# Causal attention beside a mixture of experts: the places of the next head group's maxima within a group

## The chip, the cores and the metric

The kernel runs on one core of a Trainium2 chip. The time is the device time of one execution in microseconds (us). Three runs of the kernel before gave 526.77 us (median), 525.68 and 532.72.

## The reference, cut to what matters

The input has 2 sequences of 1024 tokens with 256 features. It is layer-normalised; causal attention with 16 heads of 16 features and an ALiBi bias, and a mixture of 16 experts (2 per token) with one shared expert, are both computed from the normalised tokens and added to the input. The attention is the part that matters here:

```python
scores = jnp.einsum('bqhd,bkhd->bhqk', q, k) * scale
bias = alibi_slopes[:, None, None] * rel
causal = pos[None, :] <= pos[:, None]
scores = jnp.where(causal[None, None], scores + bias[None], NEG)
attn = jax.nn.softmax(scores, axis=-1)
out = jnp.einsum('bhqk,bkhd->bqhd', attn, v).reshape(b, s, d)
out = out @ out_w.T + out_b
```

The softmax subtracts the exact maximum of each query's row of scores. So the scores are computed twice: once for the maxima, once (transposed) for the exponentials.

## The kernel before, in words

The first 235 us or so are projections, routing and experts. Then comes the attention, which works in 8 **groups** of 4 heads (2 sequences with 4 groups each). All that the change touches lies in this part, in the bodies of the eight groups.

**A group's scores.** A group is 12 steps, one per pair of a query half (512 queries) and a key block (128 keys): steps 0 to 3 have the first half, steps 4 to 11 the second. Each step has 4 heads, so there are 48 head steps; I write 9.2 for head 2 of step 9. `exp_scores` (line 1226) issues for each the matmul of line 1234 into one of three PSUM banks, and on a diagonal block the mask matmul of line 1237 too. ScalarE takes the exponential (line 718) and frees the bank, so TensorE can be at most three head steps ahead of it. The blocks on the diagonal get narrower: 512, 384, 256 and 128 columns in steps 0 to 3 and again in steps 8 to 11; steps 4 to 7 are full, 512 columns without a mask.

**A group's weighing.** After the last head of steps 2, 4, 6, 8 and 10, `weigh` (line 1240) multiplies the exponentials of the two steps before with the values (line 1248). I call these W2 to W10: W8 weighs steps 6 and 7, W10 weighs steps 8 and 9. The last two steps of a group are weighed either after step 0 of the next group or, at the end of each pair of groups, right behind step 11.

**The maxima of the next group.** While group g is being scored, TensorE also computes the plain scores of group g+1 in 27 pieces, p0 to p26 (`max_scores`, line 1205; matmuls of line 1222, mask of line 1223). Pieces p3 to p6 are 384 wide, p7 to p10 512, p11 to p14 640, p15 to p18 768, p19 to p22 896 and p23 to p26 1024; p0 to p2 hold several short rows. VectorE reduces each to its maximum (line 970). There are two places in PSUM for pieces, so piece n waits until VectorE has read piece n-2. The 28th item, p27, is the transpose of all the maxima (line 1213), which I call T. It waits for the maximum of p26. VectorE negates its result and splits it into three bf16 parts (lines 978 to 985), SyncE's queue stores these as three more rows of the queries (`store_neg`, line 454), and the first score of group g+1 waits until they have landed (`pe.wait_ge(s_nl[par], ...)` in `pair`).

**What sets the order.** `schedule()` makes one list, `ORDER`, which TensorE and VectorE both follow. It puts the 48 head steps in a row, each with a cost of its columns and 230 more. The pieces get places in three windows, given as shares of the group's total cost: p3 to p10 of group g+1 in the first, p11 to p27 of group g+1 in the second, and p0 to p2 of group g+2 in the third. VectorE's own list holds only the pieces in their order, so it doesn't change when the shares do.

Of the kernel before, what the change touches and what calls it, by code (L numbers as in the profile page):

```python
# [57 lines left out]
NP = len(PIECES) + 1  # L58
NBUF = 4
RING = 6  # L60
EARLY = 3


def schedule():
# [6 lines left out]
    pieces = []  # L71
    for (ahead, ps), (start, end) in WINDOWS:
        cost = [(1 + PIECES[p][0]) * P * PIECES[p][2] + 200 if p < NP - 1 else 100 for p in ps]
# [3 lines left out]
    for item, cost in zip(items, exp_cost):  # L77
# [4 lines left out]
        while pieces and pieces[0][0] <= now:  # L82
# [3 lines left out]


FIRST_HALF = 11
WINDOWS = [((1, range(EARLY, FIRST_HALF)), (0.0, 0.2)), ((1, range(FIRST_HALF, NP)), (0.22, 0.88)),
           ((2, range(EARLY)), (0.9, 1.0))]  # L90
OUT_AFTER = 3
ORDER = schedule()

# [1234 lines left out]
```

## Time and profile before

| | |
|---|---|
| three runs | 526.77 us median (525.68 to 532.72) |
| the profiled execution | 528.23 us, its span 526.4 us |
| TensorE busy | 457.2 us, 87% of the span |
| VectorE busy | 324.8 us, 62% |
| ScalarE busy | 246.4 us, 47% |
| GpSimd busy | 198.5 us, 38% |
| first score of group 0 | 241.90 us |
| first score of group 7 | 466.17 us |

The busy time of TensorE counts a matmul until its modelled end, which lies up to 0.16 us after the next one has begun. So a wait shorter than that doesn't show as idle time; it shows as a larger distance between two starts. A matmul of 512 columns that is followed at once by another has its successor 0.22 us later, though its own row says 0.38.

### The profile page before, as it was taken

To read this page: it belongs to the slowest core of one execution; us is meant where nothing else is said; L and a number is where in the kernel's file an instruction comes from. 1 tells how busy PE (TensorE), PEld (TensorE's weight loads), DVE (VectorE), ACT (ScalarE), POOL (GpSimd) and SP (SyncE) were. 2 spreads that over 40 slices of the span, in tenths; PEclk is the share of its full clock that TensorE was granted. 3 is DMA by queue.
4 is the path that set the end of the run, shared out by engine and by line. 5 is a ranking of instruction groups with operands and counts; after the bars stand their busy time and mean duration, and the time that the engine had idled before them with its cause. 6 is when DMAs were issued, how large, how long until landed. Compare 5 with 4: busy or idle time off the path is not lost.

```text
span 526.4 us, 9031 instructions
## 1 busy us (share of the span) xinstructions
PE 457.2 (87%) x3049; PEld 274.7 (52%) x3050; DVE 324.8 (62%) x610; ACT 246.4 (47%) x567; POOL 198.5 (38%) x239
## 2 busy tenths in 40 slices
PE   4595999639778999978989999799998999989998
PEld 4454888416545666754444354344444444332676
DVE  4869985413344656576767768677686767744232
ACT  2620652112122333324757668486675757768300
POOL 3470777699940000008888888600000000000000
PEclk9699799978779999996999999999999999999999
DMA  8898998799997333424114333221120000010022
GB/s 279 187 403 254 324 323 284 238 159 168 201 187 180 116 116 123 131 71 136 42 44 118 103 84 106 65 80 46 53 77 16 3 2 3 1 12 7 3 87 75
DMA packets 65704, 64.60 MB, mean 123 GB/s; under 512 B 21934, under 2 KB 59538, under 8 KB 65634
## 3 DMA queue, kind: packets, MB, share of 16 engines
q1 hardware_dynamic: 51506, 47.85, 30.8%
q0 software_dynamic: 13056, 15.83, 14.3%
q10 hardware_dynamic: 1104, 0.41, 0.3%
q8 instruction: 24, 0.39, 0.3%
q14 instruction: 14, 0.11, 0.1%
HBM read 37.27 MB, written 27.13 MB: 122 GB/s over the span
## 4 chain that ended last, share of the span: by engine, by line
PE 66%; DMA 15%; DVE 10%; issue 2%; SPq 2%; POOL 2%; ACT 2%; POOLq 0%; DVEq 0%
PE ps L1248 11%; PE ps L1234 11%; PE ps L1222 11%; PE ps L1147 7%; PE ps L1043 6%; DMA x_in<-sorted_tokens 6%; PE ps L1268 5%; PE ps L1163 4%; DVE mx L970 4%; DMA ks<-aux_rows 2%; SPq L454 2%; PE ps L1237 2%; PE ps L1223 2%; PE ps L1137 2%; DMA qs<-nr 2%
## 5 line engine op out<-in xcount | busy, mean ns | idle before, releaser
L718 ACT ACTIVATE pt<-ps 128x512 f32<-128x512 f32 (+3 forms) x384 | 163.9, 496 | 86.7 <-PE ps L1237 66.9
L970 DVE TENSOR_REDUCE mx<-ps 128x1 f32<-128x384 f32 (+6 forms) x189 | 153.9, 863 | 59.3 <-PE ps L1223 59.0
L1248 PE MATMUL ps<-pt,vg 128*32 128x512 f32 (+3 forms) x768 | 72.1, 492 | 0.0
L575 POOL DMA_INDIRECT yg<-sorted_outputs,slot_i x32 | 32.0, 999 | 95.7 <-DMA sorted_outputs<-y_out 86.9
L1147 PE MATMUL ps<-w_gu,hx 128*128 x192 | 57.8, 428 | 4.4 <-issue 3.3
L1234 PE MATMUL ps<-qs,ks 111*128 111x512 bf16 (+3 forms) x192 | 55.2, 332 | 4.4 <-DMA qs<-nr 4.4
L1234 PE MATMUL ps<-qk 111*128 111x512 bf16 (+3 forms) x192 | 54.1, 328 | 3.9 <-DMA qk<-nr 2.8
L935 DVE COPY y_out<-ps 128x256 f32<-128x256 f32 x48 | 20.4, 425 | 53.9 <-PE ps L1163 48.8
L1237 PE MATMUL ps<-cbf 128*128 128x128 bf16 x256 | 52.4, 221 | 0.0
L1222 PE MATMUL ps<-qk 108*128 108x512 bf16 (+3 forms) x192 | 50.1, 328 | 0.8 <-DVE mx L970 0.6
L691 ACT ACTIVATE hx<-ps 128x384 f32<-128x384 f32 (+1 forms) x48 | 22.9, 478 | 59.2 <-PE ps L1137 56.5
L1223 PE MATMUL ps<-cbf 128*128 128x128 bf16 x224 | 47.7, 225 | 0.0
L1147 PEld LDWEIGHTS ps<-w_gu,hx 128*128 128x128 f32 x192 | 36.3, 210 | 14.0 <-issue 9.4
L542 POOL DMA_INDIRECT sorted_tokens<-xn,slot_i x32 | 32.9, 1027 | 25.1 <-DVE slot_i L877 15.7
L1222 PE MATMUL ps<-ks,qs 108*128 108x512 bf16 (+3 forms) x144 | 39.4, 341 | 1.3 <-DVE nrf L980 0.7
L547 POOL COPY vg<-v_sb 128x512 f32<-128x512 f32 x8 | 4.9, 622 | 93.1 <-PE ps L1248 93.1
L1248 PEld LDWEIGHTS ps<-pt,vg 128*32 128x32 f32 x768 | 19.6, 109 | 32.9 <-ACT pt L718 17.7
L1163 PE MATMUL ps<-w_dn,hx 128*128 x96 | 33.4, 431 | 1.3 <-ACT hx L691 0.9
L1234 PEld LDWEIGHTS ps<-qk 111*128 111x128 bf16 x192 | 17.9, 97 | 25.3 <-issue 7.8
L590 POOL TENSOR_SCALAR yg<-yg,gates 128x256 f32<-128x256 f32 x32 | 30.0, 939 | 1.2
L686 ACT ACTIVATE te_h<-ps 128x128 f32<-128x128 f32 x48 | 13.3, 278 | 34.7 <-PE ps L1147 34.7
L1268 PE MATMUL ps<-wo_t,ot 128*128 128x256 f32 x128 | 28.3, 381 | 1.3 <-DVE ot L1031 1.3
(175 smaller groups left out, 732.1 us busy)
## 6 DMA issues: line engine op xcount, KB each, us to landing
sorted_tokens<-y_out SPq DMA_DIRECT2D x12, 512.0 KB, 5.0
qk_parts<-parts SPq DMA_DIRECT2D x16, 384.0 KB, 3.5
x_in<-sorted_tokens SPq DMA_DIRECT2D x48, 128.0 KB, 2.3
sorted_outputs<-y_out SPq DMA_DIRECT2D x48, 128.0 KB, 1.7
w_gu<-e_gu SPq DMA_DIRECT2D x1, 2816.0 KB, 13.4
x_sb<-x SPq DMA_DIRECT2D x4, 512.0 KB, 8.4
w_dn<-e_dn SPq DMA_DIRECT2D x1, 2048.0 KB, 8.5
y<-x_sb SPq DMA_DIRECT2D x16, 128.0 KB, 1.7
```

The source lines that it names most:

```text
L542: g_.indirect_dma_start(out=xsd, out_offset=bass.IndirectOffsetOnAxis(ap=slot_i[:, k, t:t + 1], axis=0), in_=xn[:, t, :], in_offset=None). ...
L575: g_.indirect_dma_start(out=yg[:, n % 4, :], out_offset=None, in_=ysd, in_offset=bass.IndirectOffsetOnAxis(ap=slot_i[:, k, t:t + 1], axis= ...
L718: sc.activation(pt[:, s % 4, j, lo:CH], bank(n % 3)[:, lo:CH], ACT.Exp).then_inc(s_exp, 1)
L970: last = v.reduce_max(dst, src, axis=AX.X)
L1147: ins = te.matmul(bank(2 + w, 2 * F), hx[:, 1 - w, 1 + c, :], w_gu[:, bass.ds(e, 1), c, :].rearrange("p o f -> p (o f)"), start=c == 0, st ...
L1163: te.matmul(bank(4 + w, D), hx[:, w, 0, :], w_dn[:, bass.ds(e, 1), :].rearrange("p o f -> p (o f)"), start=True, stop=True).then_inc(s_dn, 1)
L1222: te.matmul(ps[:, at + c:at + e], q, k_buf[g % NBUF][0:K_MAX, j, c:e], start=True, stop=e < w)
L1223: ins = te.matmul(ps[:, at + w - P:at + w], idb, mask_q, start=False, stop=True)
L1234: ins = te.matmul(out[:, lo:CH], k_buf[g % NBUF][0:K_EXP, j, kb * P:(kb + 1) * P], q_buf[g % NBUF][0:K_EXP, j, qc * CH + lo:(qc + 1) * CH] ...
L1237: ins = te.matmul(out[:, lo:lo + P], idb, mask_k, start=False, stop=True)
L1248: ins = te.matmul(ps[32 * j:32 * j + 32, OUT_BANK * CH + lo:(OUT_BANK + 1) * CH], vg[:, par, kb, j, :], pt[:, s % 4, j, lo:CH], start=kb = ...
L1268: ins = te.matmul(bank(4 + m % 4, D), ot[:, n // QT * 4 + hg, n % QT * P:(n % QT + 1) * P], wo_t[:, hg, :], start=hg == 0, stop=hg == 3)
```

## The change

The three windows get other shares. The first is 0.0 to 0.18 in place of 0.0 to 0.2, the second 0.2 to 0.8 in place of 0.22 to 0.88, the third 0.84 to 0.98 in place of 0.9 to 1.0. Nothing else is edited; the number and the order of the pieces are the same, and so is each engine's work.

```diff
-WINDOWS = [((1, range(EARLY, FIRST_HALF)), (0.0, 0.2)), ((1, range(FIRST_HALF, NP)), (0.22, 0.88)),
-           ((2, range(EARLY)), (0.9, 1.0))]
+WINDOWS = [((1, range(EARLY, FIRST_HALF)), (0.0, 0.18)), ((1, range(FIRST_HALF, NP)), (0.2, 0.8)),
+           ((2, range(EARLY)), (0.84, 0.98))]
```

Only TensorE's list of instructions differs. The first place is the transpose T at the end of a group's pieces. On TensorE before, from the last piece p26 on (p26, head steps 9.2 and 9.3, T, head step 10.0):

```order
L1222 MATMUL ps<-ks,qs 128x512 [waits max_slot_freed]
L1222 MATMUL ps<-ks,qs 128x512
L1223 MATMUL ps<-cbf 128x128
L1234 MATMUL ps<-qs,ks 128x384 [waits exp_done]
L1237 MATMUL ps<-cbf 128x128
L1234 MATMUL ps<-qs,ks 128x384 [waits exp_done]
L1237 MATMUL ps<-cbf 128x128
L1213 MATMUL ps<-ident,mx 32x128 [waits max_slot_freed]
L1234 MATMUL ps<-qs,ks 128x256 [waits exp_done]
L1237 MATMUL ps<-cbf 128x128
```

The same place now (p26, head step 8.3, W8, T, head step 9.0):

```order
L1222 MATMUL ps<-ks,qs 128x512 [waits max_slot_freed]
L1222 MATMUL ps<-ks,qs 128x512
L1223 MATMUL ps<-cbf 128x128
L1234 MATMUL ps<-qs,ks 128x512 [waits exp_done]
L1237 MATMUL ps<-cbf 128x128
L1248 MATMUL ps<-pt,vg 32x512 [waits exp_done]
L1248 MATMUL ps<-pt,vg 32x512 x3
L1248 MATMUL ps<-pt,vg 32x512 [waits exp_done]
L1248 MATMUL ps<-pt,vg 32x512 x3
L1213 MATMUL ps<-ident,mx 32x128 [waits max_slot_freed]
L1234 MATMUL ps<-qs,ks 128x384 [waits exp_done]
L1237 MATMUL ps<-cbf 128x128
```

T stands four head steps earlier, and the weighing W8 now stands between p26 and T.

The second place is the stretch behind the weighing W6. On TensorE before (p21, two head steps, p22, two head steps, p23):

```order
L1222 MATMUL ps<-qk2 128x512 [waits max_slot_freed]
L1222 MATMUL ps<-qk2 128x384
L1223 MATMUL ps<-cbf 128x128
L1234 MATMUL ps<-qs,ks 128x512 [waits exp_done] x2
L1222 MATMUL ps<-qk2 128x512 [waits max_slot_freed]
L1222 MATMUL ps<-qk2 128x384
L1223 MATMUL ps<-cbf 128x128
L1234 MATMUL ps<-qs,ks 128x512 [waits exp_done] x2
L1222 MATMUL ps<-qk2 128x512 [waits max_slot_freed]
L1222 MATMUL ps<-qk2 128x512
L1223 MATMUL ps<-cbf 128x128
```

The same place now (p22, one head step, p23, two head steps, p24; a row of the list with two buffers of another group):

```order
L1222 MATMUL ps<-qk 128x512 [waits max_slot_freed]
L1222 MATMUL ps<-qk 128x384
L1223 MATMUL ps<-cbf 128x128
L1234 MATMUL ps<-qs,ks 128x512 [waits exp_done]
L1222 MATMUL ps<-qk 128x512 [waits max_slot_freed]
L1222 MATMUL ps<-qk 128x512
L1223 MATMUL ps<-cbf 128x128
L1234 MATMUL ps<-qs,ks 128x512 [waits exp_done] x2
L1222 MATMUL ps<-qk 128x512 [waits max_slot_freed]
L1222 MATMUL ps<-qk 128x512
L1223 MATMUL ps<-cbf 128x128
```

One piece more lies ahead of W6, and behind it one gap between pieces has one head step instead of two.

## Rows read from the trace of the kernel before

**Rows 1.** The page: busy time by engine, and the granted clock in 40 slices.
```profile
PE 457.2 (87%) x3049; PEld 274.7 (52%) x3050; DVE 324.8 (62%) x610; ACT 246.4 (47%) x567; POOL 198.5 (38%) x239
...
PEclk9699799978779999996999999999999999999999
```

**Rows 2.** The waits of TensorE: us in total, times, longest.
```profile
PE ps L1213 <- DVE mx L970: 8.1, 7, 1.2
PE ps L1234 <- DMA qs<-nr: 4.4, 4, 2.1
...
PE ps L1234 <- DMA qk<-nr: 2.8, 3, 1.8
```

**Rows 3.** Timeline of TensorE, group 3's end: start, length, work, idle before.
```profile
361.80 1.92 PE L1248 MATMUL ps<-pt,vg 128*32 128x512 f32 x16
363.65 0.60 PE L1222 MATMUL ps<-ks,qs 108*128 108x512 bf16 x2
...
364.15 0.33 PE L1234 MATMUL ps<-qk 111*128 111x384 bf16 x1
...
365.32 0.33 PE L1234 MATMUL ps<-qk 111*128 111x384 bf16 x1
365.48 0.22 PE L1237 MATMUL ps<-cbf 128*128 128x128 bf16 x1
366.86 0.27 PE L1213 MATMUL ps<-ident,mx 128*32 128x128 f32 x1 [1.16 <-DVE mx L970]
...
368.54 1.71 PE L1248 MATMUL ps<-pt,vg 128*32 128x512 f32 x16
370.18 0.23 PE L1234 MATMUL ps<-qk 111*128 111x128 bf16 x1
...
371.09 0.91 PE L1248 MATMUL ps<-pt,vg 128*32 128x256 f32 x16
372.24 0.39 PE L1234 MATMUL ps<-qs,ks 111*128 111x512 bf16 x1 [0.23 <-DMA qs<-nr]
```

**Rows 4.** Timeline of TensorE: T, then the next group's first score, for groups 1, 3 and 7.
```profile
269.74 0.27 PE L1213 MATMUL ps<-ident,mx 128*32 128x128 f32 x1 [1.15 <-DVE mx L970]
275.35 0.39 PE L1234 MATMUL ps<-qs,ks 111*128 111x512 bf16 x1 [1.30 <-DMA qs<-nr]
...
333.76 0.27 PE L1213 MATMUL ps<-ident,mx 128*32 128x128 f32 x1 [1.15 <-DVE mx L970]
339.90 0.39 PE L1234 MATMUL ps<-qk 111*128 111x512 bf16 x1 [1.83 <-DMA qk<-nr]
...
461.59 0.27 PE L1213 MATMUL ps<-ident,mx 128*32 128x128 f32 x1 [1.16 <-DVE mx L970]
466.17 0.39 PE L1234 MATMUL ps<-qk 111*128 111x512 bf16 x1 [0.81 <-DMA qk<-nr]
```

**Rows 5.** Maxima on VectorE: four merged rows of timelines, one row of the groups by form.
```profile
364.35 2.36 DVE L970 TENSOR_REDUCE mx<-ps 128x1 f32<-128x1024 f32 x2 [1.55 <-PE ps L1223]
...
380.19 1.55 DVE L970 TENSOR_REDUCE mx<-ps 128x1 f32<-128x640 f32 x2 [1.54 <-PE ps L1223]
...
383.93 2.69 DVE L970 TENSOR_REDUCE mx<-ps 128x1 f32<-128x768 f32 x3 [0.54 <-PE ps L1223]
...
389.94 3.22 DVE L970 TENSOR_REDUCE mx<-ps 128x1 f32<-128x896 f32 x3 [1.33 <-PE ps L1223]
...
L970 DVE TENSOR_REDUCE mx<-ps 128x1 f32<-128x1024 f32 x4 | 4.7, 1216 | 1.5 <-PE ps L1223 1.5
```

**Rows 6.** Timeline of ScalarE: exponentials of steps 9 and 11 in group 4.
```profile
396.06 0.87 ACT L718 ACTIVATE pt<-ps 128x384 f32<-128x384 f32 x2 [1.86 <-PE ps L1237]
...
401.99 0.45 ACT L718 ACTIVATE pt<-ps 128x128 f32<-128x128 f32 x2 [1.48 <-PE ps L1237]
```

**Rows 7.** Stretches: length, busy PE, PEld, DVE, ACT, POOL, granted clock, DMA share, GB/s.
```profile
241.90:249.36 7.46, 7.46 (x47) 4.17 (x51) 4.79 (x9) 5.00 (x11) 6.62 (x8) 0.70 0.37 126
307.65:313.39 5.74, 5.58 (x47) 3.12 (x51) 4.74 (x9) 5.34 (x12) 4.99 (x6) 1.00 0.43 100
```

## The prediction

> **What bounds the kernel now.** I read the page first: TensorE is busy 87% of the span, every other engine 62% or less, and the clock granted to it is full in the last 20 slices, where seven of the eight attention groups lie [rows 1]. So what counts in the attention is TensorE's own list and the places where it stops. The list of waits names two kinds that matter [rows 2]. Seven times the transpose T waits for VectorE's last maximum, 8.1 us together. Seven times a group's first score waits for the negated maxima to land, 4.4 + 2.8 = 7.2 us; of these 2.1 us belong to group 0, whose maxima the change doesn't touch, so 5.1 us are in play.
>
> Then I read TensorE's timeline by the distance between starts, since idle time is counted only from a matmul's modelled end [rows 3]. Head step 9.3 starts at 365.32, its mask at 365.48. The mask's 128 columns take 0.06, so TensorE is free at 365.54, and T begins at 366.86: the stop is 1.32 us, not 1.16. In the same way the landing waits of groups 1 to 7 cost up to 0.16 us more each than their idle time.
>
> From the same rows come the durations of back-to-back work. Piece p25 (1024 columns and a 128 mask) takes 364.15 - 363.65 = 0.50; at the same rate per column the pieces of 896 take 0.45 and those of 768 0.39. A head step of 512 columns takes 0.22, with a mask on 512 columns 0.28, on 384 columns 0.22, on 256 columns 0.17 and on 128 columns 0.12. W8 takes 363.65 - 361.80 = 1.85 and W10 370.18 - 368.54 = 1.64. Ahead of each weighing TensorE loses 0.1 more.
>
> VectorE follows at its own pace [rows 5]. Two maxima of 1024 take 2.36 us and one alone 1.22, so in a queue each takes 1.14, and 0.08 comes on top once. Taken off in the same way, a queued maximum of 640 takes 0.74, of 768 0.87 and of 896 1.00 (the last row holds two of 896 and one of 1024). A maximum starts 0.20 us after its piece ends (p25 ends at 364.15, VectorE starts at 364.35). It ended p26 at 364.35 + 2.36 = 366.71, so T follows 0.15 behind [rows 3, 5]. For a piece I take a lag of 0.06, an estimate from the distances of starts where a piece waits today; with T's 0.15 each wait below would be 0.09 longer.
>
> **The change part by part.** VectorE, ScalarE, GpSimd and SyncE get the same lists; only where TensorE puts its 27 pieces and T among the head steps changes. No DMA is issued more, less or in another order. I cut each of the seven groups that compute maxima (0 to 6) at T.
>
> *From a group's first score to T.* Two things leave this part. First the stop of 1.32 us: behind p26 now come head step 8.3 (0.28) and W8 (0.1 + 1.85), 2.23 us, before T. Second, the four head steps 9.0 to 9.3, 4 x 0.22 = 0.88 us, move behind T. That the stop goes entirely must be worked out, because the denser pieces leave VectorE further behind. From the end of W6, time zero (TensorE does p22, 7.0, p23, 7.1, 7.2, p24, 7.3, 8.0, p25, 8.1, 8.2, p26):
>
> - p22 ends 0.45; its maximum runs 0.65 to 1.73. Head step to 0.67, p23 ends 1.17; its maximum runs 1.65 to 2.87. Two head steps to 1.61.
> - p24 needs p22's place, free at 1.73 + 0.06 = 1.79: **a wait of 0.18**. It ends 2.29; maximum 2.79 to 4.01. Two head steps to 2.79.
> - p25 needs 2.87 + 0.06: **0.14**. It ends 3.43; maximum 3.93 to 5.15. Two head steps to 3.99.
> - p26 needs 4.01 + 0.06: **0.08**. It ends 4.57; maximum 5.07 to 6.29. Head step and W8 end at 6.80, and T could have begun at 6.44. So T doesn't wait, with 0.36 us to spare.
>
> The stretch from W4 to W6 has p17, two head steps, p18, one, p19, two, p20, one, p21, two. The same working gives **0.16** before p19 and **0.31** before p21. These five waits are 0.87 us; before, the same method gives 0.27 (0.18 at p18, 0.05 at p19, 0.04 at p23), and the starts in the trace agree with it. Near the start of the group p9 comes one head step earlier: **0.23** more. New waits on VectorE are thus 0.60 + 0.23 = 0.83, say 0.85 us per group. Bounds: none (W2, W4 and W6 hide them, as they hide nearly all now) and twice as much. I take the worked value, because the same recurrence gives the stops that the trace has now.
>
> Sum of this part per group: -1.32 - 0.88 + 0.85 = -1.35; for seven groups **-9.5 us**.
>
> *From T to the next group's first score.* Today this part is as long as the negation, the store and the landing: the seven distances are 5.61 (group 1), 5.35, 6.14, 5.38, 5.10, 5.08 and 4.58 us (group 7), of which three stand in [rows 4]; together 37.2. Now it holds more TensorE work: T 0.11, step 9 0.88, p0 0.46, step 10 4 x 0.17, p1 and p2 2 x 0.33, W10 0.1 + 1.64, step 11 4 x 0.12, in all 5.0 us. And ScalarE begins to bind, because T's stop, in which it caught up, is gone. Two exponentials of 384 take 0.87 us, one of them 0.49 alone and 0.38 in the queue; two of 128 take 0.45, 0.28 and 0.17 [rows 6]. Counted from T: 9.2 is scored at 1.23, its exponential runs 1.45 to 1.94 and that of 9.3 1.84 to 2.33; head step 10.2 needs the latter's bank and TensorE is there at 2.12, so **0.27**. After W10, at 4.81, four short head steps come in a row: 11.0 ends at 4.93, its exponential at 5.43, and 11.3, which needs its bank, waits from 5.17 to 5.49, **0.32**. Before, p0, p1 and p2 lay so that ScalarE had the time. The part then takes 5.66 us with 0.05 more at the very end, and 6.56 where steps 10 and 11 are weighed right behind it (ahead of groups 2, 4 and 6; 0.8 to 0.9 and 0.1, the row at 371.09 in [rows 3]). The landing no longer decides except in group 3, where it took 6.14. Sum: 4 odd groups at 5.66, 6.14, 5.66, 5.66 and 3 even ones at 6.56, together 42.8. The part grows by **5.6 us**. Bounds: without any wait on ScalarE it is 39.6 (+2.4), with twice the waits about +9.7.
>
> *Everything else.* Groups' ends, the last group (no pieces, same list) and the projections cost nothing, since no instruction there moves. First-piece waits on loaded q and k rows: those loads are issued a whole group or more before; SyncE's queue has nothing in flight when T comes 1 to 2 us earlier, so store_neg is as quick as now.
>
> **Sum:** -9.5 + 5.6 = **-3.9 us**. The profiled execution, 528.23 us (span 526.4), becomes 524.3. The median of the runs, 526.77, lies 1.5 lower and becomes 522.9.
>
> **A rule that speaks against it.** TensorE has never left the full clock once the attention is under way, although it stops twice in every group and often for a tenth of a microsecond between pieces [rows 1, 7]. The Trainium skill (TensorE: Matmul & The Clock Gate, section "A second HAM failure mode: psum-queue depth-cycling") says that a kernel which cycles through PSUM banks can stop TensorE briefly so often that its clock swings between the two levels. By that rule the sum would have the price of the third rival below; the trace so far contradicts it for stops like these.
>
> **The rivals.** *First, the new waits don't come.* VectorE and ScalarE keep up, and only T's stop and the landing waits go: 7 x -2.20 + 2.4 = -13.0, 513.8 us. For it speaks that VectorE idles 1.54, 0.54 and 1.33 us at the weighings [rows 5]; against it that two places in PSUM let it be only two pieces behind, however long it idles later. *Second, it comes out even.* ScalarE's waits are twice mine (+4.1), because T's stop is also what let it catch up in step 9: 0 to +2, 526.8 to 528.8 us. For it speaks that the group's end holds 12 narrow head steps and hardly any piece; against it that ScalarE's pace there is less than TensorE's pace with W10 counted. *Third, slower:* the many short stops from p15 to p26 bring the clock down to 1.2 GHz. Price: group 0 began at 0.70 of full clock over 7.46 us, so some 4.5 us of it at 1.2 GHz, and the same 47 matmuls took 5.74 in group 2 [rows 7]: 1.72 us lost for 4.5. If the packed stretch of 17 us ran so, a group would lose 6.5 us, seven groups 45: 568 us. It decides from the first such group on; more than two of them (14.4 us) make the kernel slower by over 2%. Against it: the stops are shorter than the 1.32 that goes. That the change doesn't do what it says is excluded by TensorE's list.
>
> **How the numbers follow.** My forecast (a gain of 1 to 8 us) gets 0.74, the first rival 0.05, the second 0.17, the third 0.04. The forecast's own range comes from half to one and a half of the two unknown terms (6 and 4 us): 522.9 less or plus 5, so 518.0 to 527.9. It takes in part of the second rival and leaves out some 2 in 10: the first, the third and the tails. I give **518.0 to 527.8**. Two per cent, 10.5 us, is about what a measurement can tell from no change; beyond it on the fast side lies most of the first rival (0.03), on the slow side the third (0.03), and within it 0.94.
>
> **What would show it.** T's row should have no idle time before it (seven waits of 1.15 gone). The landing waits of groups 1 to 7 should be gone but for some 0.5 us at group 3. L1222 should wait for VectorE with visible idle time before pieces of 896 and 1024, and L1234 for ScalarE in steps 10 and 11. A group should shrink from about 32 us by 0.5. The forecast is wrong if T still waits (VectorE further behind than worked), or if the head steps behind T are not slowed by ScalarE.

## The result and the profile after

| | before | after |
|---|---|---|
| median of 22 runs | 528.77 us (524.09 to 534.62) | 524.92 us (521.16 to 530.14) |
| profiled execution's span | 526.4 us | 523.2 us |

The ratio of after to before is 0.9943, with a 95% interval of 0.9918 to 0.9967: 3 us faster by the ratio (0.0057 x 528.8), where 3.9 had been forecast. The ratio leaves out the executions that were over 1.5% above the fastest of their kernel; the medians have them in. In a later comparison on one chip with three other kernels the same kernel had 0.9968 (0.9924 to 1.0011), so the size of the gain is known only roughly from whole runs. The groups of the trace tell it more sharply.

The page's rows for the engines and the clock after the change (columns as in [rows 1]):

```profile
PE 461.9 (88%) x3049; PEld 271.6 (52%) x3050; DVE 324.3 (62%) x610; ACT 249.4 (48%) x567; POOL 198.4 (38%) x239
...
PEclk9799799977779999997999999999999999999999
```

The work of VectorE is the same to within half a microsecond, and the clock is full in the attention but for the first 3 us of group 0 (4 us before). TensorE's waits by line after the change, and the row of L1222 in the kernel before:

```profile
PE ps L1234 <- DMA qs<-nr: 3.0, 2, 2.8
PE ps L1222 <- DVE mx L970: 2.5, 14, 0.4
...
PE ps L1234 <- ACT pt L718: 0.3, 1, 0.3
PE ps L1234 <- DMA qk<-nr: 0.2, 1, 0.2
```

```profile
PE ps L1222 <- DVE mx L970: 0.9, 6, 0.2
```

Compared with [rows 2], the row of L1213 (8.1 us, 7 times) is gone. The landing shows 3.0 + 0.2 us in place of 4.4 + 2.8, and 2.8 of that is group 0. VectorE now stops L1222 visibly 14 times, 2.5 us, where it had been 6 times, 0.9 us. Six of the 14 are the old ones, 0.15 each at p5. Seven are new, 0.16 each at p21. The longest, 0.45, lies ahead of group 0 at 239.27, where the change moves nothing and the clock was down.

TensorE's timeline in group 3: p21, then from p22 on (it answers [rows 3]):

```profile
354.01 0.55 PE L1222 MATMUL ps<-ks,qs 108*128 108x512 bf16 x2 [0.16 <-DVE mx L970]
...
356.84 0.55 PE L1222 MATMUL ps<-ks,qs 108*128 108x512 bf16 x2
...
358.00 0.60 PE L1234 MATMUL ps<-qk 111*128 111x512 bf16 x2
358.63 0.60 PE L1222 MATMUL ps<-ks,qs 108*128 108x512 bf16 x2
...
359.77 0.60 PE L1222 MATMUL ps<-ks,qs 108*128 108x512 bf16 x2
...
360.90 0.60 PE L1222 MATMUL ps<-ks,qs 108*128 108x512 bf16 x2
...
361.40 0.38 PE L1234 MATMUL ps<-qk 111*128 111x512 bf16 x1
361.62 0.22 PE L1237 MATMUL ps<-cbf 128*128 128x128 bf16 x1
361.77 1.92 PE L1248 MATMUL ps<-pt,vg 128*32 128x512 f32 x16
363.62 0.28 PE L1213 MATMUL ps<-ident,mx 128*32 128x128 f32 x1
...
365.74 0.22 PE L1237 MATMUL ps<-cbf 128*128 128x128 bf16 x1
366.01 0.28 PE L1234 MATMUL ps<-qk 111*128 111x256 bf16 x1
...
366.79 1.71 PE L1248 MATMUL ps<-pt,vg 128*32 128x512 f32 x16
...
368.67 0.22 PE L1234 MATMUL ps<-qk 111*128 111x128 bf16 x1
368.73 0.22 PE L1237 MATMUL ps<-cbf 128*128 128x128 bf16 x1
369.09 0.23 PE L1234 MATMUL ps<-qk 111*128 111x128 bf16 x1
...
370.10 0.39 PE L1234 MATMUL ps<-qs,ks 111*128 111x512 bf16 x1
```

T at 363.62 stands right behind W8 (361.77 + 1.85) with no wait. The two head steps from 358.00 should be over at 358.44, and p24 starts at 358.63: the stop of 0.19 that the working put at 0.18. In the same way p25, at 359.77, waits 0.13 (worked 0.14), and p21, at 354.01, waits 0.32 (worked 0.31), of which the view shows 0.16. One of ScalarE's stops is at head step 11.3: 11.2's mask starts at 368.73 and takes 0.06, and 11.3 starts at 369.09, so 0.30 (worked 0.32). The other is at head step 10.2: the mask before it starts at 365.74, and 10.2 at 366.01, so 0.21 (worked 0.27).

T and the next group's first score for groups 1, 3 and 7 (they answer [rows 4]):

```profile
268.82 0.28 PE L1213 MATMUL ps<-ident,mx 128*32 128x128 f32 x1
274.74 0.39 PE L1234 MATMUL ps<-qs,ks 111*128 111x512 bf16 x1 [0.16 <-DMA qs<-nr]
...
331.75 0.28 PE L1213 MATMUL ps<-ident,mx 128*32 128x128 f32 x1
337.97 0.39 PE L1234 MATMUL ps<-qk 111*128 111x512 bf16 x1 [0.25 <-DMA qk<-nr]
...
457.55 0.28 PE L1213 MATMUL ps<-ident,mx 128*32 128x128 f32 x1
462.96 0.39 PE L1234 MATMUL ps<-qk 111*128 111x512 bf16 x1
```

From these starts (line 1213 and each group's first line 1234) I take for every kernel two sums over the seven groups, the part up to T and the part from T on. They are the two halves of the prediction.

| kernel | up to T | from T on | groups 0 to 6 |
|---|---|---|---|
| before | 187.0 | 37.2 | 224.3 |
| after | 177.3 | 42.8 | 220.0 |
| after, the second time | 177.4 | 42.9 | 220.3 |
| second window alone | 177.1 | 44.3 | 221.4 |
| third window as before | 177.9 | 42.8 | 220.7 |
| T ahead of W8 | 175.3 | 55.6 | 230.8 |
| T behind W10 | 203.1 | 32.9 | 235.9 |
| before, halved maxima | 179.0 | 37.9 | 216.9 |
| after, halved maxima | 168.5 | 46.4 | 214.9 |
| after, early copy | 177.5 | 43.1 | 220.6 |
| other windows, early copy | 178.0 | 40.8 | 218.8 |
| table | 171.2 | 44.7 | 215.9 |
| table, early copy | 171.1 | 42.8 | 213.9 |
| table, early copy, the second time | 170.9 | 42.8 | 213.8 |

The groups lost 4.2 us (-9.8 and +5.5). The first score came 1.0 us later in this execution (242.92, 241.90 before), so the span shows 3.2. The first part of the program isn't touched by the change: first scores lay between 238.4 and 244.1 us over all fourteen profiles. That scatter alone can make whole runs of one kernel differ by several microseconds.

### The profile page after: what moved, and what is told of

Read it like the earlier page. It is cut to its first block, busy times and chain, and to the rows that moved or that the text cites. A ratio compares the mean times of both kernels' runs of the same rounds, so it can differ in the third digit from the quotient of the medians.

```text
span 523.2 us, 9031 instructions
## 1 busy us (share of the span) xinstructions
PE 461.9 (88%) x3049; PEld 271.6 (52%) x3050; DVE 324.3 (62%) x610; ACT 249.4 (48%) x567; POOL 198.4 (38%) x239
## 3 DMA queue, kind: packets, MB, share of 16 engines
HBM read 37.27 MB, written 27.13 MB: 123 GB/s over the span
## 4 chain that ended last, share of the span: by engine, by line
PE 66%; DVE 13%; DMA 12%; issue 2%; ACT 2%; POOL 2%; SPq 1%; POOLq 0%; DVEq 0%
PE ps L1248 12%; PE ps L1222 10%; PE ps L1234 10%; PE ps L1147 7%; PE ps L1268 5%; DMA x_in<-sorted_tokens 5%; DVE mx L970 5%; PE ps L1043 4%; PE ps L1163 4%; DMA ks<-aux_rows 2%; PE ps L1237 2%; PE ps L1223 2%; PE ps L1137 2%; ACT pt L718 2%; DMA x_sb<-x 1%
## 5 line engine op out<-in xcount | busy, mean ns | idle before, releaser
L718 ACT ACTIVATE pt<-ps 128x512 f32<-128x512 f32 (+3 forms) x384 | 167.1, 494 | 79.7 <-PE ps L1237 55.2
L1222 PE MATMUL ps<-qk 108*128 108x512 bf16 (+3 forms) x192 | 50.2, 328 | 1.8 <-DVE mx L970 1.3
L542 POOL DMA_INDIRECT sorted_tokens<-xn,slot_i x32 | 32.8, 1024 | 25.0 <-DVE slot_i L877 15.6
L1222 PE MATMUL ps<-ks,qs 108*128 108x512 bf16 (+3 forms) x144 | 38.5, 335 | 2.4 <-DVE mx L970 1.2
L1137 PE MATMUL ps<-ident,x_in 128*128 128x128 f32 x96 | 20.0, 292 | 12.0 <-DMA x_in<-sorted_tokens 11.9
```

The source lines that it names most:

```text
L542: g_.indirect_dma_start(out=xsd, out_offset=bass.IndirectOffsetOnAxis(ap=slot_i[:, k, t:t + 1], axis=0), in_=xn[:, t, :], in_offset=None). ...
L718: sc.activation(pt[:, s % 4, j, lo:CH], bank(n % 3)[:, lo:CH], ACT.Exp).then_inc(s_exp, 1)
L1137: ins = te.transpose(ps[:, v * CH + (1 + c) * P:v * CH + (2 + c) * P], x_in[:, u, c * P:(c + 1) * P], ident[:, :])
L1222: te.matmul(ps[:, at + c:at + e], q, k_buf[g % NBUF][0:K_MAX, j, c:e], start=True, stop=e < w)
```

## The experiments

### Which window counts, and is T's place behind W8 the reason

**The second window alone.**

```diff
 WINDOWS = [((1, range(EARLY, FIRST_HALF)), (0.0, 0.2)),
-           ((1, range(FIRST_HALF, NP)), (0.22, 0.88)), ((2, range(EARLY)), (0.9, 1.0))]
+           ((1, range(FIRST_HALF, NP)), (0.2, 0.8)), ((2, range(EARLY)), (0.9, 1.0))]
```

> Only the second window is changed (0.2 to 0.8); the first and the third are as before. Theory (T's stop goes because W8 and the head steps before it cover VectorE's last maximum): the distance from a group's first score to T shrinks by 10 us or a little more over seven groups against before, as with the whole change, since the second window alone moves T behind W8; the part from T on grows by some 5, because T comes four head steps earlier. In all 5 us less than before, about 1 us less than the whole change (p9 keeps its place, and p0 to p2 stand at the very end). Rival (the denser first window or the earlier p0 to p2 bring the gain): no gain here, the time of before.

Measured: ratio 0.9939 (0.9869 to 1.001), groups 221.4 us. The shrinking of the part up to T is wholly there (-9.9). But the groups don't take 1 us less than with the whole change, they take 1.4 more: p9's place made no difference up to T, since p11 waits 0.27 here where p9 waits 0.23 there, and from T on it took 44.3. Whole runs don't tell this kernel from the whole change. The rival, that the other windows bring the gain, falls.

**The third window as before.**

```diff
-           ((2, range(EARLY)), (0.84, 0.98))]
+           ((2, range(EARLY)), (0.9, 1.0))]
```

> The whole change but for the third window, which is as before (0.9 to 1.0), so that p0 to p2 stand among steps 10 and 11. Tells what the third window is worth. Theory: the part up to T is that of the changed kernel (177.3 us over seven groups); behind T ScalarE's waits only change their place (one of 0.33 at head step 9.3 in place of those at 10.2 and 11.3), so 42 to 44.5 us, the upper end if the landing decides in the odd groups as it did when only the second window was changed. Rival (p0 to p2 relieve ScalarE's waits at 11.3, which the change brought): 2 us faster than the changed kernel.

Measured: ratio 0.9922 (0.9886 to 0.9958), from T on 42.8, as after. The third window is worth nothing that I can see. The list behind T is that of the kernel above, which had 44.3; its excess lies at groups 1, 3 and 7 (6.75, 6.49 and 5.80 us from T, here 6.09, 6.15 and 5.45). For all three its trace names the landing. So the landing differs by half a microsecond between two kernels that are alike behind T, and in the odd groups it is still close to deciding (two causes are named below, under the prediction). In this kernel group 3 also waited 0.5 us for GpSimd (see below).

**T ahead of W8.**

```diff
 ORDER = schedule()
+T_AT, W_AT = ORDER.index(("max", 1, NP - 1)), ORDER.index(("out", 8))
+ORDER[W_AT], ORDER[T_AT] = ORDER[T_AT], ORDER[W_AT]
```

> The changed kernel with T and the weighing W8 exchanged, so that T comes right behind p26 and head step 8.3. Theory: T stops again, for 1.6 us in each of seven groups (its worked earliest start 6.44 less 4.85), 11 us together, and the landing never decides; 6 us slower than before, 10.5 slower than the whole change. Rival (T's stop isn't a cost of its own, whatever is moved ahead of T is only paid elsewhere): the time of the whole change, within 2 us.

TensorE's timeline of this kernel at T in group 3 (its T is line 1215):

```profile
364.06 0.38 PE L1236 MATMUL ps<-qk 111*128 111x512 bf16 x1
364.28 0.22 PE L1239 MATMUL ps<-cbf 128*128 128x128 bf16 x1
365.91 0.27 PE L1215 MATMUL ps<-ident,mx 128*32 128x128 f32 x1 [1.41 <-DVE mx L972]
```

The stop is 365.91 - 364.34 = 1.57 us (worked 1.59), and its seven idle times are 9.9 us. The groups take 230.8 us, 10.8 more than after, and the ratio to before is 1.0123 (1.0058 to 1.0187). So it is the weighing behind p26 that covers VectorE's last maxima. The denser pieces without it would have made the kernel slower.

**T later, behind W10.**

```diff
+LATE = [x for x in ORDER if x[0] == "max" and x[1:] in ((1, NP - 1), (2, 0), (2, 1), (2, 2))]
+ORDER = [x for x in ORDER if x not in LATE]
+W_AT = ORDER.index(("out", 10)) + 1
+ORDER[W_AT:W_AT] = LATE[:2]
...
```

> The kernel before with T moved later, behind W10, so that step 10 and W10 cover VectorE's last maxima, and p0 to p2 among the head steps of step 11. Theory (T's stop and the landing lie on one path, so covering the stop by a later T gains nothing): T doesn't stop, but each group's first score now waits 2 to 3 us for the landing, and a group gets 1.8 us longer: 12 us slower than before. Rival A (only T's stop matters): 8 us faster. Rival B (a stop as long as that also brings TensorE's clock down, as it did once behind a stop of 2.67 us when the maxima were halved): 6 to 10 us more than the 12.

T and the first score of group 3, then of group 5, in this kernel; then two stretches right behind these first scores (columns as in [rows 7]):

```profile
340.49 0.28 PE L1219 MATMUL ps<-ident,mx 128*32 128x128 f32 x1
345.12 0.39 PE L1240 MATMUL ps<-qk 111*128 111x512 bf16 x1 [1.75 <-DMA qk<-nr]
...
406.37 0.29 PE L1219 MATMUL ps<-ident,mx 128*32 128x128 f32 x1
411.00 0.39 PE L1240 MATMUL ps<-qs,ks 111*128 111x512 bf16 x1 [1.75 <-DMA qs<-nr]
```

```profile
411.00:415.00 4.00, 3.96 (x24) 1.89 (x28) 2.14 (x4) 2.33 (x4) 0.00 (x0) 0.61 0.00 0
345.10:349.10 4.00, 3.83 (x38) 2.04 (x39) 2.36 (x5) 2.92 (x6) 0.60 (x1) 1.00 0.25 63
```

T doesn't stop, yet the groups take 235.9 us, 11.7 more than before, and the ratio is 1.013 (1.0056 to 1.0205). The theory holds: from T to the next group's first score the negation, the store and the landing need 4.6 us at the least, so a later T pays at the group's start. Rival A, 8 us faster, falls. Behind the stop at 411.00 the clock was down (0.61 over 4 us: 24 matmuls instead of 38). Behind an equal stop at 345.12 it wasn't. Groups 1 and 5 took 30.29 and 30.12 us up to T, group 3, which stands at the same place of its pair, 28.73. So rival B's price is in the 11.7 with 3.0 us, in two of the seven groups, and the late T alone costs some 9 instead of the 12 worked. In group 6, which has no p0 to p2 behind its T, the stop at the end was 3.53 us, and group 7 began at the lower clock; from its first score to the end of the program it took 61.95 us where the kernel before took 60.26. These 1.7 us lie outside the table. The profiled execution took 541.94 us and the five lay between 536.49 and 546.29, so how often the clock falls may differ between executions.

### Is it VectorE's work that sets the stops

Both kernels take the maxima of p3 to p26 over the right half of the scores only; they leave out the left half.

```diff
                 dst = mx[:, par, :].rearrange("p (j t) -> p j t", j=HG)[:, j0:j0 + nj, qt]
+                src = src[:, :, w // 2:w] if nj == 1 else src
                 last = v.reduce_max(dst, src, axis=AX.X)
```

> The kernel before, with each maximum of p3 to p26 taken over the right half of its scores only (so the maxima are not the true ones). VectorE's queued maxima take about half. Theory (VectorE's reductions set T's stop and the waits between pieces): T's stop shrinks from 1.32 to about 0.6 us, the waits of pieces nearly vanish (0.85 to 0.1 per group), a group is 1.4 us shorter, 9 to 10 us less than before in all. Rival (the stops are a lag of signals, not of work): less than 3 us gained.

> The changed kernel with the same halved maxima. Theory: the waits at p5, p9, p10, p15, p19, p21, p24, p25 and p26 (1.7 us per group) go, T doesn't stop in either; 11 to 12 us less than the changed kernel, the part from T to the next group's first score stays at 42.8 us over seven groups, since ScalarE and TensorE's own work set it. Rival (ScalarE takes over as soon as VectorE is quick): 5 us or less gained.

In the undisturbed groups 4 to 6 the part up to T fell from 26.11 and 26.96 to 24.70 and 25.59 in the kernel before (-1.4 each, as worked), and from 24.80 and 25.65 to 23.07 and 23.95 in the one after (-1.7, as worked). T's idle time fell from 8.1 to 3.0 us. So the stops are VectorE's work and not a lag of signals. The totals fell by less than expected: 7.4 us where 9 to 10 had been expected, and 5.1 where 11 to 12 had. The 5.1 alone would nearly fit the second run's rival, that ScalarE takes over, but ScalarE's stops at head steps 10.2 and 11.3 are 0.21 and 0.30 us in both kernels. In the one after, the part from T on grew by 3.6 us, 2.1 of them ahead of group 3 and the rest ahead of groups 1, 2 and 7. And in both kernels group 3 found something new. Its first score, and two stretches of the halved kernel before: right behind it, and as many matmuls at the start of group 5:

```profile
334.47 0.38 PE L1235 MATMUL ps<-qk 111*128 111x512 bf16 x1 [2.67 <-POOL vg L547]
```

```profile
334.50:340.00 5.50, 5.50 (x40) 2.61 (x41) 1.76 (x5) 3.25 (x6) 2.33 (x4) 0.69 0.31 78
396.60:400.60 4.00, 3.99 (x40) 2.19 (x41) 1.93 (x6) 3.16 (x7) 0.61 (x1) 1.00 0.00 0
```

GpSimd copies group 3's values only when it has gathered and added all 32 rows of the experts' outputs, at 334.4 us here. TensorE was there 2.67 us earlier. Behind this stop its clock was down for a while, and the part of group 3 up to T took 27.13 us where group 1 took 25.59: 1.5 more. The kernel after, halved, stopped 2.61 us for GpSimd at the same place and paid the same 1.5 (25.46 us up to T, 23.96 in group 1).

### How near that new wait is, and what lies beyond

**After, with the copy earlier.**

```diff
                 if n == K_TOP * TT // 2:
                     copy_next(0)
+                if n == 22:
+                    copy_next(1)
...
-            copy_next(1)
             for g in range(NG - 2):
```

> The changed kernel with GpSimd's copy of group 3's values at the 22nd gathered row. In the changed kernel's trace the copy ended at 337.26 us and group 3 began at 337.97, in that of the variant with the third window as before group 3 waited 0.5 us for it. Theory (the change has used up this cover): the same time as the changed kernel within 1 us, and no wait for GpSimd. Rival (the copy already sets group 3's start): 1 us or more faster.

> The changed kernel once more, on one chip with the next three. 3 to 4 us less than before; the part up to T 177.3 us over seven groups, from T on 42.8; the landing may move the latter by 1 us.

Measured: ratios 0.9957 (0.9916 to 0.9997) and 0.9968 (0.9924 to 1.0011), groups 220.6 and 220.3. No difference, as expected. The changed kernel's copy on GpSimd shows how little was left, beside group 3's first score at 337.97:

```profile
336.65 0.61 POOL L547 COPY vg<-v_sb 128x512 f32<-128x512 f32 x1
```

It ends 0.7 us ahead (337.26 and 337.97). The kernel before had 3.5 us (336.42 and 339.90).

**A table of places.** From the five worked waits I drew the guess that a piece should stand right before a weighing, since the weighing then covers two maxima. A search with the same durations as in the prediction gave a table for all pieces: p16, p21 and p26 right before W4, W6 and W8, and T right behind W8.

```diff
 ORDER = schedule()
+AT = [1, 2, 3, 4, 5, 6, 8, 9, 12, 14, 16, 20, 23, 24, 25, 27, 30, 31, 34, 35, 36, 39, 42, 44, 45, 48, 51, 58]
+WORK, MAXIMA = [x for x in ORDER if x[0] != "max"], [x for x in ORDER if x[0] == "max"]
+ORDER = []
+for k in range(len(WORK) + 1):
+    ORDER += [m for m, at in zip(MAXIMA, AT) if at == k] + WORK[k:k + 1]
```

> Every piece gets its own place, from a table: p16, p21 and p26 stand right before W4, W6 and W8, T right behind W8, p3 to p6 one head step apart. Theory (a weighing covers two maxima if the piece before it has just been scored): waits on VectorE fall from 1.7 to 0.4 us per group, the part up to T takes 169 us over seven groups, 8 less than in the changed kernel, and from T on 41 to 44 us. But group 3 then begins some 3 us before GpSimd has copied its values at about 337 us, waits for that, and the clock may fall for 3 us behind it (1.5 us): 4 to 6 us less than the changed kernel. Rival (VectorE is the bound and any order gives the same): no gain.

> The same table, and GpSimd copies group 3's values in its loop over the gathered rows (at the 22nd of 32) and not behind it. Theory: group 3's wait goes, 8 to 10 us less than the changed kernel, 12 less than before. Rival (GpSimd's copy isn't what group 3 waits for): the time of the table alone.

Group 3's first score with the table alone, and with the early copy:

```profile
335.43 0.38 PE L1239 MATMUL ps<-qk 111*128 111x512 bf16 x1 [1.93 <-POOL vg L552]
```

```profile
334.77 0.39 PE L1240 MATMUL ps<-qk 111*128 111x512 bf16 x1 [1.53 <-DMA qk<-nr]
```

The table alone has 0.9789 (0.9729 to 0.9849), with the early copy 0.9741 (0.9685 to 0.9796). Up to T it takes 171 us, 6 less than after (8 expected). GpSimd's wait was there with the table alone, 1.93 us, but the clock stayed full behind it. The early copy removed the wait, and at once the landing decided in group 3 (6.9 us from T). It gained 2.0 us in the groups.

**Other windows, with the early copy.**

```diff
-WINDOWS = [((1, range(EARLY, FIRST_HALF)), (0.0, 0.18)), ((1, range(FIRST_HALF, NP)), (0.2, 0.8)),
-           ((2, range(EARLY)), (0.84, 0.98))]
+WINDOWS = [((1, range(EARLY, FIRST_HALF)), (0.0, 0.2)), ((1, range(FIRST_HALF, NP)), (0.2, 0.82)),
+           ((2, range(EARLY)), (0.86, 1.0))]
```

> Only the three windows again (0.0 to 0.2, 0.2 to 0.82, 0.86 to 1.0), with the early copy: W8 stands between p26 and one head step before T. Theory: waits on VectorE 1.4 instead of 1.7 us per group, ScalarE's at 11.3 gone since p2 stands in step 11, so 2 to 3 us less than the changed kernel; the landing takes back up to 1 of them. Rival (only a table by hand gets below the changed kernel): no difference.

> The table with the early copy once more, beside the changed kernel on one chip: 6 us less than the changed kernel, 9 to 13 less than before. Rival (its lead came from a quick first part of the program): the same time as the changed kernel.

Measured: 0.9893 (0.9826 to 0.9961) for the windows, 0.9773 (0.9694 to 0.9851) for the table with the early copy, 521.59 and 516.72 us beside 525.90 for the changed kernel on the same chip. In the groups the windows gain 1.5 us and the table 6.5 on the changed kernel; 2 to 3 and 6 had been expected. The windows' profile also has a loss outside the table. Two stretches of its group 7, which began at 457.23 (columns as in [rows 7]):

```profile
467.50:471.50 4.00, 3.81 (x27) 0.99 (x17) 1.62 (x3) 4.00 (x10) 0.00 (x0) 1.00 0.11 10
471.50:475.00 3.50, 3.50 (x17) 0.58 (x16) 0.44 (x1) 0.91 (x2) 0.00 (x0) 0.51 0.00 0
```

The clock fell although TensorE had been busy, and had not visibly stopped for longer than 0.34 us since group 7 began. From that group's first score to the end this kernel took 61.97 us, the kernel before 60.26. What brought it down stays open. The table with the early copy beats both kernels, by 2.3 to 2.6% the one before.

## Why the prediction was right, and where it wasn't

- **T's stop goes, behind W8.** Right, in the mechanism too. T has no wait, and with W8 behind T instead of ahead of it a stop of 1.57 us is back, where 1.59 was worked.
- **New waits between pieces.** Right in place and in size: 0.32, 0.19 and 0.13 at p21, p24 and p25. Only p21's shows as idle time; the forecast had said visible stops before pieces of 1024 too. The part up to T lost 1.30 us in each of groups 1 to 6 (worked 1.35), and 1.94 in group 0; 9.8 us together, 9.5 forecast. Group 0 began later, with some 3.1 us of it at the lower clock instead of 4.4, which I take for its excess. No run tests it; the kernel with the third window as before, with 4.5 us of group 0 at the lower clock, took 26.54 us up to T there, the changed kernel 25.90.
- **From T to the next group.** The sum is right, 42.8 us forecast and measured, +5.5 against +5.6. Two of its seven terms are off and cancel. Group 1 took 5.92 instead of 5.66, because the landing still decided. Group 7 took 5.41 instead of 5.66, because group 6 has no p0 to p2 of a further group to score, which I had overlooked. It gains only 0.25 of their 1.12 us: without them TensorE waits for ScalarE at head steps 9.3, 10.0, 10.1, 10.2 and 11.3, for 0.30, 0.16, 0.21, 0.21 and 0.30 us. The bounds of this part were summed unevenly: without the two worked waits (0.59 us) in six groups it is 39.3 us and not 39.6, and with twice the waits it grows by 9.1 and not 9.7. The forecast's own range doesn't rest on them.
- **"The landing no longer decides except in group 3."** Too strong. It decided in groups 1 and 3 of the changed kernel (0.16 and 0.25 us of idle time), and in other kernels with nearly the same list behind T by up to 0.8 more. The premise behind it, that store_neg is as quick as now, failed: where the landing decided, group 1 began 5.92 us behind T in place of 5.61, and group 7, the second time, 5.50 in place of 4.58. The traces show two things that lengthen this path, though no run changes either by itself. First, VectorE's last two steps for group 3 and for group 7 in the changed kernel:

```profile
332.70 0.66 DVE L983 CAST nr<-nrf 32x128 bf16<-32x128 f32 x1
333.39 0.48 DVE L985 TENSOR_TENSOR nr<-nrf,nr 32x128 bf16<-32x128 f32 x1
...
458.50 0.21 DVE L983 CAST nr<-nrf 32x128 bf16<-32x128 f32 x1
458.75 0.28 DVE L985 TENSOR_TENSOR nr<-nrf,nr 32x128 bf16<-32x128 f32 x1
```

Ahead of groups 4 to 7, with GpSimd's gathering over, the last step ends 1.46 to 1.48 us behind T in all fourteen profiles. Ahead of groups 1 to 3, while GpSimd mostly works beside it, it ends up to 2.25 us behind T. Second, a DMA packet of 16 KB that takes about 1 us, on a queue that the profile calls instruction. Group 7's first score with the second window alone (its T is at 457.65), and that queue's row for the stretch in which the three stores run, 460.3 to 462.0:

```profile
463.45 0.39 PE L1234 MATMUL ps<-qk 111*128 111x512 bf16 x1 [0.42 <-DMA qk<-nr]
...
q8 instruction: 1, 0.02, 3.2%
```

The kernel before has no such row in the same stretch behind its T (464.2 to 465.9): its packet had come at 462.7, before the stores. There the first score followed T by 4.58 us, here by 5.80. In groups 4 to 7 of the fourteen profiles TensorE stood visibly idle before the first score 21 times; the profile names the landing for 17 of them and ScalarE for the rest. In the 7 in which no such packet ran beside a store the first score followed T by 4.58 to 4.65 us, in the other 14 by 5.10 to 5.88. With the table, group 3's landing (6.9 and 7.1 us) had both, and GpSimd's gathering traffic beside it; how much each costs there stays open.

- **Everything else costs nothing.** Right for this change. But the cover of GpSimd's copy, which I hadn't named at all, shrank from 3.5 to 0.7 us. A change with twice the gain would have met it.
- **The clock.** The third rival didn't come: from 246 us on the clock stayed full to the end, through 13 visible stops of L1222, of 0.15 or 0.16 us each. The Trainium skill's rule on brief stops while cycling through PSUM banks (TensorE: Matmul & The Clock Gate, section "A second HAM failure mode: psum-queue depth-cycling") doesn't describe this kernel. In the other kernels above the clock fell six times after group 0, five times at a single stop at a group's start and once, with other windows, without a long stop; whether that one is of the skill's kind, no run shows.
- **The level.** 522.9 us had been forecast, with a range of 518.0 to 527.8, from a median of three runs, 526.77; the median of 22 was 528.77 before and 524.92 after. That their difference is 3.9 us, just as forecast, is partly luck: by the ratio of the comparison it is 3.0 us, and by the groups 4.2.

## What to carry to other kernels

When one engine must wait for the last result of another, look for work of the first that is due anyway and long enough, and put exactly that between the last input and the wait; then work out with queue times what the denser order does further up. A wait that ends in a store and a landing has two ends: moving the waiting instruction later only moves the stop. And before a stage is made faster, list who else must be ready at its end, and by how much each is early today, since that margin is what the gain uses up.

## What the hardware showed that I had not expected

After group 0, and not counting the program's last microsecond, TensorE's clock fell six times in the fourteen profiles, and each fall cost 1.4 to 1.7 us. Five of the falls came at a stop at a group's start, of 1.75, 1.76, 2.61, 2.67 and 3.53 us. Other stops at the same places, of 1.53, 1.68, 1.75, 1.83 and 1.93 us, had none. Two stops of the same 1.75 us, at the same place of two groups of one kernel, differed in this. So a stop of this size has a second price that comes or doesn't, and the runs don't show on what that depends. The sixth fall came in the middle of group 7 without such a stop, so not every fall is the price of one.

A small store's landing is not a fixed time either. From T to the waiting score, over VectorE's four steps and three stores, it took 4.6 us where no 16 KB packet of another queue ran beside a store, and 5.1 to 5.9 us where one did.
